# Cross-attention and FFN on one core: who transposes the normalised tokens of the FFN tiles

## The reference, cut to what matters

```python
# x: (8, 1024, 512) f32, ctx: (8, 64, 384) f32, 16 heads of 32
x = x + xattn(layernorm(x), ctx, Wq, bq, Wk, bk, Wv, bv, Wo, bo)
xn = layernorm(x)                                  # over the 512 channels
hidden = xn @ W1 + b1                              # 512 -> 2048
wave = w_imag * sin(phases + 0.1 * hidden)
gain = cos(phases) * w_real + sin(phases) * w_imag
act = relu(hidden + gain * wave * 0.1)
x = x + act @ W2 + b2                              # 2048 -> 512
```

## Time and profile before

| | us |
|---|---|
| median of 3 runs (2108.9 to 2115.45) | 2113.91 |
| the profiled execution | 2114.67 |
| its span, first to last instruction | 2112.9 |
| PE busy | 2082.1 (99%) |
| DVE / ACT / POOL busy | 1313.1 / 1142.7 / 1041.3 |

### The profile page before, as it was taken

How to read it: one execution, slowest core, us unless ns; L and a number is a source line. 1 busy time by engine, 2 the same in 40 slices (tenths; PEclk the granted TensorE clock), 3 DMA queues, 4 the chain that set the end, 5 groups by cost and what they waited for, 6 DMA issues and landing times.

```text
span 2112.9 us, 27349 instructions
## 1 busy us (share of the span) xinstructions
PE 2082.1 (99%) x9986; PEld 1743.2 (83%) x9986; DVE 1313.1 (62%) x1994; ACT 1142.7 (54%) x2036; POOL 1041.3 (49%) x757
## 2 busy tenths in 40 slices
PE   7999999999999999999999999999999999999999
PEld 5888888888887878888888888888888888888887
DVE  4888898888876755555455555555545555455554
ACT  4666667667664655444454544445444444545543
POOL 3777777777775434353343533435334353443421
PEclk9999999999999999999999999999999999999999
DMA  5122222232213310101001010110101101011000
GB/s 180 56 87 99 81 97 100 84 101 79 76 55 120 100 41 11 41 0 41 21 21 40 1 40 3 38 41 1 41 1 41 40 1 40 1 40 40 1 20 21
DMA packets 54264, 102.49 MB, mean 49 GB/s; under 512 B 4841, under 2 KB 5353, under 8 KB 54129
## 3 DMA queue, kind: packets, MB, share of 16 engines
q1 hardware_dynamic: 52976, 100.17, 14.0%
q10 hardware_dynamic: 1152, 0.56, 0.1%
HBM read 66.10 MB, written 34.62 MB: 48 GB/s over the span
## 4 chain that ended last, share of the span: by engine, by line
PE 89%; DVE 4%; ACT 3%; issue 2%; DMA 1%; POOL 0%; SPq 0%; POOLq 0%; ACTq 0%; DVEq 0%
PE psum L1044 28%; PE psum L1046 28%; PE psum L1045 28%; PE psum L1125 2%; PE psum L1050 2%; ACT turns L756 1%; ACT hid L758 1%; DVE hid L990 1%; DMA ctx_sb<-in_ctx 0%; DVE prob L897 0%; DVE top L903 0%; DMA stage<-in_w 0%; ACT act_hi L747 0%; DVE total L883 0%; PE psum L1081 0%
## 5 line engine op out<-in xcount | busy, mean ns | idle before, releaser
L585 POOL TENSOR_TENSOR frac<-turns,frac 128x512 f32<-128x512 f32 x256 | 332.9, 1300 | 856.9 <-DVE frac L1018 856.9
L990 DVE SCALAR_TENSOR_TENSOR hid<-frac,gain,hid 128x512 f32<-128x512 f32 x256 | 319.4, 1248 | 148.0 <-ACT frac L743 146.7
L1044 PE MATMUL psum<-w_hi,act_hi 128*128 128x512 f32 x1024 | 400.6, 391 | 0.0
L1046 PE MATMUL psum<-w_hi,act_lo 128*128 128x512 f32 x1024 | 399.2, 390 | 0.0
L1045 PE MATMUL psum<-w_lo,act_hi 128*128 128x512 f32 x1024 | 398.9, 390 | 0.0
L756 ACT ACTIVATE turns<-psum,u_shift 128x512 f32<-128x512 f32 x256 | 176.4, 689 | 371.2 <-PE psum L1046 329.6
L747 ACT ACTIVATE act_hi<-hid 128x512 fp32r<-128x512 f32 x256 | 161.8, 632 | 346.0 <-DVE hid L990 346.0
L1018 DVE TENSOR_SCALAR frac<-turns 128x512 f32<-128x512 f32 x256 | 110.3, 431 | 322.9 <-ACT turns L756 322.9
L993 DVE SCALAR_TENSOR_TENSOR act_lo<-hid,act_hi 128x512 fp32r<-128x512 f32 x256 | 197.0, 769 | 178.7 <-ACT act_hi L747 178.7
L1046 PEld LDWEIGHTS psum<-w_hi,act_lo 128*128 128x128 f32 x1024 | 192.5, 188 | 40.4
L1044 PEld LDWEIGHTS psum<-w_hi,act_hi 128*128 128x128 f32 x1024 | 192.7, 188 | 39.8 <-issue 0.3
(11 more groups left out here) (143 smaller groups left out, 4198.2 us busy)
## 6 DMA issues: line engine op xcount, KB each, us to landing
res<-in_x SPq DMA_DIRECT2D x64, 256.0 KB, 2.8
x_dram<-res SPq DMA_DIRECT2D x64, 256.0 KB, 2.0
x_sb<-x_dram SPq DMA_DIRECT2D x16, 1024.0 KB, 5.6
x_sb<-in_x SPq DMA_DIRECT2D x15, 1024.0 KB, 5.8
out<-x_sb SPq DMA_DIRECT2D x15, 1024.0 KB, 4.2
stage<-in_w SPq DMA_DIRECT2D x32, 256.0 KB, 2.7
v_in<-v_dram SPq DMA_DIRECT2D x16, 128.0 KB, 3.0
x_sb<-in_x SPq DMA_DIRECT2D x4, 256.0 KB, 4.0
```

The costliest lines, as they stand in the source:

```text
L585: pool.tensor_tensor(frac[:, j % 2, :], turns[:, j % 2, :], frac[:, j % 2, :], ALU.subtract)\
L990: dve.scalar_tensor_tensor(out=hid[:, j % 2, :], in0=frac[:, j % 2, :], scalar=gain[:, f:f + 1], in1=hid[:, j % 2, :], op0=ALU.mult, op1=A ...
L1044: pe.matmul(o, a_hi, b_hi, start=first, stop=False)
L1046: return pe.matmul(o, a_lo, b_hi, start=False, stop=last)
```

## The change

The transposes of FFN tiles 1 to 15 leave TensorE. Only tile 0 of the FFN, and the attention phase, keep them. Instead:

1. ACT writes `xn` in another layout: per partition 16 channel groups x 4 token blocks x 32 channels.
2. DVE transposes 32x32 squares of it into `stage`, in two halves of 128 x 1024 elements (token blocks 0, 1 and token blocks 2, 3), at the end of chunks 10 and 12 (11 and 12 in the first tile, where `stage` is still in use for weights).
3. For each half SP issues 16 SBUF-to-SBUF transfers, which move each 32-partition square row to its partitions, back into `xn`. One transfer is 32 partitions x 4 runs of 256 B, 32 KB. The second DVE transpose waits for the first half's transfers, since both go through `stage`.
4. In chunk 15 ACT waits for both halves and makes `xt_hi` from `xn` in SBUF, with runs of 32 elements; DVE makes `xt_lo` from `xn` and `xt_hi`, both in SBUF.
5. `LN_AT` goes from 7 to 5, so each step of the layer norm is two chunks earlier.
6. TensorE's wait for `hid` is also made in chunks 0 to 3 of later tiles.

```diff
-LN_AT = 7
+LN_AT = 5
+TURN_AT = 10
+TURNS = NB * NB
...
+        SQ = 32
+        xn_squares = xn[:].rearrange("p n c -> p (n c)").rearrange("p (q n j) -> p n q j", n=NB, j=SQ)
+        to_turn = xn[:].rearrange("p n c -> p (n c)").rearrange("p (q h x) -> p h q x", h=2, q=KC * NB)
+        turned = stage[:].rearrange("p s c -> p (s c)").rearrange("p (q x) -> p q x", q=KC * NB)
+        squares_out = stage[:].rearrange("p s c -> p (s c)").rearrange("p (k b x) -> p k b x", k=KC, b=NB)
+        squares_in = xn[:].rearrange("p n c -> p (n c)").rearrange("p (k a h x) -> p h k a x", k=KC, a=NB, h=2)
+        channels = xn[:].rearrange("p n c -> p (n c)").rearrange("p (k a n i) -> p k n a i", k=KC, a=NB, i=SQ)
...
+        def turn_at(t, half):
+            return TURN_AT + 2 * half + (half == 0 and t == 0)
...  SP, before the wait for the finished tile
+                for half in range(2):
+                    sp.wait_ge(turn_done, 2 * t + half + 1)
+                    for a in range(NB):
+                        for b in range(NB):
+                            sp.dma_start(squares_in[b * SQ:(b + 1) * SQ, half, :, a, :],
+                                         squares_out[a * SQ:(a + 1) * SQ, :, b, :]).then_inc(turned_in[half], 16)
...  ACT, chunk 15
+                    for half in range(2):
+                        act.wait_ge(turned_in[half], 16 * TURNS * (t + 1))
                     for k in range(KC):
-                        xt_to_hi(TILES + t + 1, k, k)
+                        act.activation(by_square(xt_hi[:, k, :]), channels[:, k], ACT.Copy).then_inc(xt_hi_done, 1)
...  DVE, chunk 15
-                        xt_to_lo(TILES + t + 1, k, k)
+                        dve.wait_ge(xt_hi_done, (TILES + t + 1) * KC + k + 1)
+                        dve.tensor_tensor(by_square(xt_lo[:, k, :]), channels[:, k],
+                                          by_square(xt_hi[:, k, :]).bitcast(F32), ALU.subtract).then_inc(xt_lo_done, 1)
...  DVE, at the end of a chunk
+                if t + 1 < TILES and f == turn_at(t, 0):
+                    dve.wait_ge(xn_half, t + 1)
+                    if t:
+                        dve.wait_ge(turned_in[1], 16 * TURNS * t)
+                    else:
+                        dve.wait_ge(w_lo_done, SPLIT0 + FFN_CHUNKS)
+                    dve.transpose(turned, to_turn[:, 0]).then_inc(turn_done, 1)
+                if t + 1 < TILES and f == turn_at(t, 1):
+                    dve.wait_ge(xn_done, TILES + t + 2)
+                    dve.wait_ge(turned_in[0], 16 * TURNS * (t + 1))
+                    dve.transpose(turned, to_turn[:, 1]).then_inc(turn_done, 1)
...  TensorE
-                    if f >= NB:
+                    if j >= NB:
                         pe.wait_ge(hid_done, j - NB + 1)
...
-                    if f == FC - 1 and t + 1 < TILES:
-                        pe.wait_ge(xn_done, TILES + t + 2)
-                        for k in range(KC):
-                            pe.wait_ge(hid_done, t * FC + FC - NB + k + 1)
-                            transposes(TILES + t + 1, k, k)
```

More of the change, by code:

```diff
@@ L265, in xattn_ffn @@
         f_psum, y2_done = sem("f_psum"), sem("y2_done")
+        turn_done, turned_in = sem("turn_done"), sems("turned_in", 2)
         rows_psum = sem("rows_psum")
@@ L328, in half_blocks, with by_square @@
             return range(part * NB // 2, (part + 1) * NB // 2)
+        SQ = 32
[5 more added lines that the diff above has]
+        channels = xn[:].rearrange("p n c -> p (n c)").rearrange("p (k a n i) -> p k n a i", k=KC, a=NB, i=SQ)
+        def by_square(tokens):
+            return tokens.rearrange("p (n a i) -> p n a i", n=NB, a=NB)
+        def turn_at(t, half):
+            return TURN_AT + 2 * half + (half == 0 and t == 0)
         block = stack.enter_context(nc.Block())
@@ L620, in layer_rows @@
                     act.wait_ge(s_psum, S_BANKS * GROUPS)
-                if T > TILES:
+                if T == TILES + 1:
                     act.wait_ge(xt_psum, KC * T)
+                if T > TILES + 1:
+                    act.wait_ge(xt_lo_done, KC * T)
                 for n in blocks:
-                    last = act.activation(normalised(T)[:, n, :], x_sb[T % XBUFS][:, n, :], ACT.Identity,
-                                          bias=shift_rows[:, T % 2, n:n + 1], scale=rstd[:, T % 2, n:n + 1])
+                    rows, to = x_sb[T % XBUFS][:, n, :], normalised(T)[:, n, :]
+                    if T > TILES:
+                        rows, to = rows.rearrange("p (q j) -> p q j", j=SQ), xn_squares[:, n]
+                    last = act.activation(to, rows, ACT.Identity, bias=shift_rows[:, T % 2, n:n + 1],
+                                          scale=rstd[:, T % 2, n:n + 1])
                 last.then_inc(xn_done if NB - 1 in blocks or T == 0 else xn_half, 1)
```

## The result

| | us |
|---|---|
| before, median of 10 runs (2108.9 to 2115.45) | 2113.94 |
| changed, median of 10 runs (2103.45 to 2110.75) | 2108.23 |
| ratio | 0.9975, 95% interval 0.9965 to 0.9984 |
| span of the profiled execution | 2107.4 |

The kernel is faster, as forecast, but by 5.7 us and not by 24.8; the time is within the 0.3% that the prediction called no change. The page of the changed kernel shows where to look: SP's queue and DMAs are in the chain that ended last, where they had no share to speak of before.

The account below looks back on a forecast made before the run. PE's queue was taken to bound the kernel. Transposes removed, -28.8, and first tile, +4, sum to -24.8: from 2114.67 to 2089.9, with the median 0.8 lower, 2089 us; range 2079 to 2132.

Parts of the forecast that it names:

- What bounds the kernel, the 2.06 us of the transposes, 14 alike boundaries: FFN tile ends: PE's queue bounds; removing transposes takes 7.73 us to 5.67, 2.06 a tile, 14 times: 28.8 us.
- Squares 1.2 us, hidden: DVE at the end of chunks 10 and 12: 1.2 us a half, hidden where DVE is free; up to 2.5.
- `xt` from SBUF: Chunk 15: four `xt_hi` on ACT take 2.06 us; DVE's `xt_lo` follow, and PE doesn't wait, 1.0 us to spare.
- Landing after the last issue 2.0: SP's transfers of each half: the last DMA lands 2.0 us after its issue, as the stores of `res`.
- Distance of two issues: SP's 16 DMAs per half: I taken as 0.53 us, bounds 0.44 and 0.75; gain gone at 0.68.
- T12 + 0.25 + 30 I: When the second half lands, counted from the start of chunk 12's `turns`; I is the distance of two issues.
- rival B: Tile boundaries: I 0.62 to 0.66 or contended `xt_lo` eats part of the gain, 14 us lost, 2103; chance 0.15.
- the sign given for it: ACT's `xt_hi` in chunk 15 waits more than 1 us on a DMA: slow transfers or a partly eaten gain.
- The first tile, +4: First FFN tile: late halves lose 2.8 us plus some clock in idle time; 4 taken, between 0 and 8.
- Layer norm earlier, at no cost: Layer norm two chunks earlier: same instructions, costs nothing; the tile's load has 5.5 us of cover.
- Rival A: ACT's wait in chunk 15: the 2 x 16 DMAs set the tile's end, 2132 to 2155 us; chance 0.31.
- The Trainium skill's rule: SP's transfers: those under 64 KB pay mostly overhead, which spoke against the change.

Follow-up runs that it names:

- the early kernel: Changed kernel with the layer norm at chunk 4 and squares after chunks 9 and 11 (first tile still 11 and 12): 2098.2 us, ratio 0.9926 to before.
- the later kernel: Changed kernel with the squares at the end of chunks 11 and 13 (first tile 11 and 12 as changed): 2214.1 us, ratio 1.0474 to before.
- the kernel that avoids both waits: Changed kernel with layer norm at chunk 4, squares after chunks 9 and 11, and FFN tile 1 still transposed by PE: 2086.7 us, ratio 0.987 to before.

## Why the prediction went wrong, step by step

- **What bounds the kernel, the 2.06 us of the transposes, 14 alike boundaries:** right. With the transfers out, the rest of the span is 28.8 us lower.
- **Squares 1.2 us, hidden:** right, 1.24. The Trainium skill's figure ("VectorE: DVE Perf Modes", The three transpose paths), taken eightfold, had given 2.5; for f32 squares the measurement decides, half of that.
- **`xt` from SBUF:** right: `xt_hi` 2.19 for four (2.06 taken), `xt_lo` 2.50 (2.9).
- **Landing after the last issue 2.0:** right, 1.9.
- **Distance of two issues:** here it failed, and this is the step that made the forecast wrong. I took I = 0.53, between the 0.44 and 0.605 of the earlier trace rows, by an argument on partitions and runs. It is 0.64, nearly whatever the shape; slow single issues make it 0.67 in the first train of the tile shown (10.1 us from its first to its last issue). Both bounds were read too low as well: I had divided the length of four issues by four, while the starts of the same rows lie 0.475 (`res`) and 0.64 (`v_in`) apart. The upper row thus had the measured value. With 0.64 the formula T12 + 0.25 + 30 I gives 19.5, past the 18.5 where PE was to begin to wait; measured 19.3 to 20.2 at twelve boundaries. The mechanism was right. This is what rival B had (0.62 to 0.66, 14 us lost at the boundaries, chance 0.15), and the sign given for it, ACT waiting over 1 us for a DMA in chunk 15, is what the trace shows (1.7 to 3.5 us). The term cost 9.3 us at twelve boundaries. Of the other 5.1, at the last two, some 3.7 are the later start of the second squares there (T12 + 8.5 and 8.1 against 6.45), which no term of the prediction covers.
- **The first tile, +4:** the second miss, 10.5 measured. Counted from each kernel's first `turns`, the second half was to land at 85.5 us (769 - 683.5) and ACT's `xt_hi` started at 93.3 (775.15 - 681.88), 7.7 later, and `second(14)` came later by as much. 4.5 of it are the two trains, 9.8 and 10.65 us from first to last issue in place of 7.95 each: the same term. 3.3 are the start of the squares, at 66.2 and not 62.9. Of these the kernel with the layer norm alone shows 2.5 (65.5 against 63.0): the two weight splits take 2.37 us and not 1.29 beside GpSimd's bias, which the earlier layer norm put there, and the chunks before are slower too. The 7.7 stand beside the 1.2 us that I had added for the clock, so 6.5 more than forecast. PE's half clock after its 7.39 us without work is hardly a further cause: PE stood 3.12 us for `xt_lo` once more behind it, so at full clock it would only have stood longer. Behind this second stand the half clock cost some 0.5 us at most: `second(14)` came 5.9 us after the start of `xt_hi`, and 5.35 in the early kernel, where it waited for `act_lo(14)` and not for PE's own matmuls.
- **Layer norm earlier, at no cost:** right for the 14 boundaries and for the total, shown by itself; in the first tile it has a share in the 3.3 us above.
- **Rival A** was given 30 us for each us of I; the later kernel shows that the price of a long wait is higher, 7.5 us for 5.44 of delay, because the clock falls with it. At the waits of the changed kernel's 14 boundaries, up to 2.0 us in all, it did not.
- **The Trainium skill's rule** on small transfers ("DMA: Bandwidth & Descriptors", Rules for kernel authors) holds in its sense: 8 KB, 32 KB and 128 KB cost the queue about the same (0.63, 0.64 and 0.69 us). The fixed 2 us a DMA is what the Trainium skill ("DMA: Bandwidth & Descriptors", Anatomy of one DMA) gives for DMAs that GpSimd issues; ours are SP's. A single one landed after 1.9 us here, but they overlap: the 32 of the tile shown went out in 23.7 us, with DVE's squares between the halves.

The forecast of 2089 was one chunk's start and one tile's path away: the kernel that avoids both waits takes 2086.7.

## What to carry to other kernels

When work is moved from the bounding engine to a chain of squares, DMAs and copies, the engine's saving is the easy part of the sum; lay out the new chain's end against the first time it is asked for, and where two trains share one buffer, the issues of both count, 30 distances here. If the unknown price is near the point that decides, start the chain earlier: one chunk was worth 14 us here and cost at most 1.8 us, in the first tile. Read the distance of two issues from start to start, and not as the length of a train over its count. Look at the first tile by itself, as its cover is another.

## What the runs showed of the hardware that I had not expected

- An SBUF-to-SBUF DMA takes SP 0.60 us and the next starts 0.64 after its start (medians 0.63 to 0.65), for 8 KB as for 32 KB, with 32, 64 or 128 partitions; 128 KB go out at 0.64 to 0.74, 32 KB from SBUF to DRAM at 0.47 to 0.48.
- Single issues of 1.0 to 1.8 us stand in such trains without a wait that the profile shows.
- A 32x32 transpose on VectorE of 128x1024 f32 takes 1.24 us, that is about what the reduction over as many elements takes (1.22).
- After PE had stood 6.1 and 7.4 us, its granted clock was 0.50 to 0.61 in the stretches of 4 and 5 us around and behind the restart, with matmuls 0.43 us apart; after the waits of 0.2 to 1.2 us of the changed kernel's boundaries it stayed 1.00.
